# An adaptive FFN on one core: block 1 conditioned inside the first product, the first ternary quarter cut in two, and the steps of the first stage put in another order

## The reference, cut to what matters

```python
w = weights[conditions]                        # (128, 64, 64), one matrix per batch row
c = jnp.einsum('bct,bcd->bdt', x, w)           # x: (128, 64, 512)
def ternarize(W):                              # W1 (2048, 512) and W2 (512, 2048)
    delta = 0.05 * max(abs(W)); mask = abs(W) > delta
    alpha = sum(where(mask, abs(W), 0)) / max(sum(mask), 1)
    return alpha * sign(W) * mask
h = gelu(c @ ternarize(W1).T + b1)             # 2048 wide
y = h @ ternarize(W2).T + b2
scale = max(abs(y)) / 7 + 1e-8                 # one scale for all of y
out = x + clip(round(y / scale), -7, 7) * scale
```

## Time and profile before

| | us |
|---|---|
| median of 3 runs | 1014.92 (1014.45 to 1015.22) |
| the profiled execution | 1013.76 |
| its span | 1012.0 |
| PE busy | 928.2 (92%) |
| DVE busy | 647.5 (64%) |
| ACT busy | 546.2 (54%) |
| POOL busy | 145.4 (14%) |

### The profile page before, as it was taken

The page is one execution under the profiler, slowest core; times in us unless marked ns, Lnnn a source line. Parts: engine busy times, 40 slices in busy tenths (PEclk is TensorE's granted clock), DMA queues, the critical chain, the costliest instruction groups (busy, mean ns, idle before and its releaser), DMA issues.

```text
span 1012.0 us, 14566 instructions
## 1 busy us (share of the span) xinstructions
PE 928.2 (92%) x5088; PEld 439.1 (43%) x5088; DVE 647.5 (64%) x1025; ACT 546.2 (54%) x688; POOL 145.4 (14%) x187
## 2 busy tenths in 40 slices
PE   2899999999999999999999999999999999999600
PEld 2354444444444444444444444444444444444200
DVE  7999666566667666665667666565666665633492
ACT  5685826455472827446372827446372826535290
POOL 1420030210303030110303030110303030000000
PEclk9999999999999999999999999999999999999855
DMA  9401201111210301121210301121210301105899
GB/s 347 136 9 38 46 11 42 47 47 41 52 41 17 76 10 41 46 47 41 52 41 10 83 10 41 45 48 41 52 41 10 75 18 42 42 0 201 300 394 391
DMA packets 24317, 77.85 MB, mean 77 GB/s; under 512 B 3952, under 2 KB 4080, under 8 KB 23792
## 3 DMA queue, kind: packets, MB, share of 16 engines
q1 hardware_dynamic: 20032, 73.41, 24.1%
q0 software_dynamic: 3840, 3.94, 1.4%
q10 hardware_dynamic: 432, 0.34, 0.1%
HBM read 60.89 MB, written 16.78 MB: 77 GB/s over the span
## 4 chain that ended last, share of the span: by engine, by line
PE 83%; issue 9%; DVE 4%; ACT 1%; DMA 1%; DVEq 0%; POOL 0%; POOLq 0%
PE ps L426 41%; PE ps L436 36%; PE ps L491 3%; PE ps L406 3%; ACT y L680 1%; DVE st L814 1%; DVE wts L1017 1%; DMA condb<-in_itok_B 1%; DVE y L1017 0%; DVE y L833 0%; PE ps L414 0%; PE ps L454 0%; DVE yc L746 0%; DVEq L58 0%; DVE st L697 0%
## 5 line engine op out<-in xcount | busy, mean ns | idle before, releaser
L426 PE MATMUL ps<-yc,wts 128*128 128x512 f16 x2048 | 446.3, 380 | 3.6 <-DVE yc L746 3.6
L436 PE MATMUL ps<-wts 128*128 128x512 f16 x1792 | 391.4, 379 | 0.0
L426 PEld LDWEIGHTS ps<-yc,wts 128*128 128x128 f16 x2048 | 200.7, 98 | 246.8 <-DVE yc L746 4.1
L730 DVE SCALAR_TENSOR_TENSOR wts<-g,st,wts 128x512 f16<-128x512 f32 x256 | 186.3, 749 | 144.0 <-ACT wts L593 142.4
L588 ACT ACTIVATE g<-ps,b1t,st 128x512 f32<-128x512 f32 x256 | 197.9, 773 | 129.0 <-PE ps L426 120.7
L436 PEld LDWEIGHTS ps<-wts 128*128 128x128 f16 x1792 | 173.4, 98 | 204.9
L593 ACT ACTIVATE wts<-g,st 128x512 f16<-128x512 f32 x256 | 180.8, 712 | 0.0
L575 ACT ACTIVATE xs<-yx,st 128x2048 f16<-128x2048 f32 x28 | 56.1, 2002 | 135.5 <-DVE st L764 135.5
L359 POOL PARTITION_ALL_REDUCE st<-st x46 | 22.7, 494 | 672.5 <-DVE st L699 412.7
L343 POOL DMA_INDIRECT wg<-in_L_cond_weights,ids x112 | 110.0, 982 | 41.5 <-issue 29.1
L735 DVE SCALAR_TENSOR_TENSOR y<-ps,st,b2b 128x512 f32 (+1 forms) x56 | 41.6, 747 | 78.9 <-PE ps L436 78.1
(11 more groups left out here) (127 smaller groups left out, 359.3 us busy)
## 6 DMA issues: line engine op xcount, KB each, us to landing
yx<-in_x SPq DMA_DIRECT2D x56, 512.0 KB, 6.2
out<-wts SPq DMA_DIRECT2D x12, 512.0 KB, 14.9
wts<-in_x SPq DMA_DIRECT2D x10, 512.0 KB, 5.6
y<-in_L_ffn_W SPq DMA_DIRECT2D x8, 512.0 KB, 8.6
wts<-in_x SPq DMA_DIRECT2D x4, 1024.0 KB, 5.2
y<-in_L_ffn_W SPq DMA_DIRECT2D x4, 1024.0 KB, 18.5
y<-in_x SPq DMA_DIRECT2D x4, 1024.0 KB, 10.7
out<-y SPq DMA_DIRECT2D x4, 1024.0 KB, 15.3
```

The lines of the kernel that those rows point to most:

```text
L426: last = nc.tensor.matmul(psH[:, j % HB, :], T1T[:, j // HC, k, j % HC * P:(j % HC + 1) * P], csp[:, a, k, :], start=(k == 0 and a == 0), ...
L436: last = nc.tensor.matmul(psY[:, r % 2, :], hsp[:, a, j, r * P:(r + 1) * P], T2T[:, j, :], start=(j == 0 and a == 0), stop=(j == HT - 1 an ...
L730: nc.vector.scalar_tensor_tensor(out=hsp[:, 1, j, :], in0=g[:, j % HB, :], scalar=s_h, in1=hsp[:, 0, j, :], op0=ALU.mult, op1=ALU.subtract ...
```

## The change

It touches the part ahead of the loop alone. On the way to the first product: the maximum of |x| of block 0, taken by DVE, becomes a sum of |x| on ACT (with the factor 2·KT of the bound turned to 2/P); all eight `absolute` stand ahead of `spread_w(0)`; two clears go ahead of the wait for the conditions; POOL gathers half of block 1's weights at once and half behind the maximum of W1; x of block 1 is loaded ahead of W2. The first ternary quarter is made in two parts, tile 0 ahead of `low_c0` and tiles 1 to 3 behind it; `ternary1(1)` and `ternary1(2)` move ahead of the chain that makes `hscale_ready`. Block 1 is conditioned on PE between tile 0 and tile 1 of the first product, and ACT copies its c out beside tiles 3 and 5, to a place of its own in y. `relu2(0)` moves from behind the 16 gelus of block 0 to behind `gelu(0, 11)`. `count2` becomes 64 matmuls with the mask as weights and one moving column, where it was 16 with 512 columns. `low_x(0, 0)` moves from ahead of the stores of y of block 0 to behind the maxima that follow them.

```diff
@@ SP
             load_direct(0)
+            load_direct(1)
             load_weight(w2s, W2.rearrange("p j n -> p (j n)"), WCH, w2_loaded)
-            load_direct(1)
@@ POOL
-            gather_direct(0)
+            gather_direct(0, range(RT))
+            gather_direct(1, range(0, 2))
             all_max(max1_part, 1, m1r, m1, max1_all)
+            gather_direct(1, range(2, RT))
+            pool.wait_ge(x0_summed, 1)
             all_max(xwb_part, 1, xwbr, xwb, xwb_all)
-            gather_direct(1)
@@ PE
             def count2(c):
-                for n in range(WCH):
-                    last = nc.tensor.matmul(psN2, twos[:, :], quarter(neg2, c, n), start=(c == 0 and n == 0),
+                for n in range(QUARTER // P):
+                    at = c * QUARTER + n * P
+                    last = nc.tensor.matmul(psN2, neg2[:, at:at + P], twos[:, 0:1], start=(c == 0 and n == 0),
...
                 first(0, j, wait_bank=j >= HB, wait_c=False)
-            pe.wait_ge(xdirect_loaded[1], 16)
-            pe.wait_ge(w_spread, 2)
-            condition_direct(1, 0, psC)
-            pe.wait_ge(g_made, HT - 2)
-            condition_direct(1, 1, psC1)
+                if j == 0:
+                    pe.wait_ge(xdirect_loaded[1], 16)
+                    pe.wait_ge(w_spread, 2)
+                    condition_direct(1, 0, psC)
+                    condition_direct(1, 1, psC0)
+            pe.wait_ge(c_copied, 2)
             pe.wait_ge(g_made, HT)
@@ ACT
+            nc.scalar.activation(dump_x, xdirect[0].rearrange("p r t -> p (r t)"), ACT.Abs, accum_out=xwb[:, 0:1])\
+                .then_inc(x0_summed, 1)
...
-            for c in range(3):
-                relu1(c)
+            relu1(0)
             high_c0(0, psC)
             high_c0(1, psC0)
+            relu1(1)
+            act.wait_ge(c_made, 2)
+            spread_w(1)
+            relu1(2)
             relu1(3)
             act.wait_ge(relu_summed, WCH)
-            hidden(0, lambda j: spread_w(1) if j == 3 else None, wait_c=False)
...
+            def beside_first(j):
+                if j in (3, 5):
+                    copy_c_direct(1, (j - 3) // 2, (psC, psC0)[(j - 3) // 2])
+                if j == 11:
+                    act.wait_ge(delta2_ready, 1)
+                    act.wait_ge(t1_made, WCH)
+                    for side in range(2):
+                        relu2(0, side)
+            hidden(0, beside_first, wait_c=False)
@@ DVE
-            mask_w1(1)
             dve.wait_ge(wd_gathered[0], 16 * RT)
-            nc.vector.tensor_reduce(xwb[:, 1:2], wg[:, 0:RT, :], AX.XY, ALU.max, apply_absolute_value=True)
-            dve.wait_ge(xdirect_loaded[0], 16)
-            nc.vector.tensor_reduce(xwb[:, 0:1], xdirect[0], AX.XY, ALU.max, apply_absolute_value=True).then_inc(xwb_part, 1)
+            nc.vector.tensor_reduce(xwb[:, 1:2], wg[:, 0:RT, :], AX.XY, ALU.max, apply_absolute_value=True).then_inc(xwb_part, 1)
+            mask_w1(1)
             mask_w1(2)
...
             mask_w1(3)
-            ternary1(0)
+            ternary1(0, slice(0, 1), t1_begun)
             dve.wait_ge(cscale_ready, 1)
             low_c0(0, psC)
             low_c0(1, psC0)
+            ternary1(0, slice(1, HC))
+            dve.wait_ge(n1_counted, 1)
+            nc.vector.tensor_reduce(n1, psN1, AX.X, ALU.add).then_inc(n_read, 1)
+            ternary1(1)
+            ternary1(2)
             dve.wait_ge(relu_summed, WCH)
             nc.vector.tensor_reduce(rs1s, rs1, AX.X, ALU.add).then_inc(sum1_part, 1)
...
-            ternary1(1)
+            ternary1(3)
             low_h(0, 0)
...
+            for c in range(WCH):
                 last = max_w2(c)
+                low_h(0, 2 * c + 1)
+                if c < WCH - 1:
+                    low_h(0, 2 * c + 2)
...
             max_y(0, r, tile_y(r), slot(r), wait_last=r > 0)
+            low_x(0, 0)
             hidden_step(0, link, False)
```

More of the change, by code:

```diff
@@ L143, in build @@
         cf = g[:, :, :]
+        cf1 = y[:, 4, :, :]
+        dump_x = hsp[:, 0, 0:RT, :].rearrange("p j r -> p (j r)")
         def place(ap):
@@ L345, in gather, with gather_direct @@
                         in_offset=bass.IndirectOffsetOnAxis(ap=ids[:, j:j + 1], axis=0)).then_inc(w_gathered[j // HALF], 16)
-            def gather_direct(b):
-                for r in range(RT):
+            def gather_direct(b, tiles):
+                for r in tiles:
                     nc.gpsimd.indirect_dma_start(
@@ L468, in _ @@
             for j in range(HT):
-                pe.wait_ge(t1_made, j // HC + 1)
+                if j == 0:
+                    pe.wait_ge(t1_begun, 1)
+                else:
+                    pe.wait_ge(t1_made, j // HC + 1)
                 if j == HB - 1:
@@ L557, in copy_c_direct @@
                 act.wait_ge(c_made, 2 * b + half + 1)
-                nc.scalar.activation(cf[:, :, half_rows(half)], bank, ACT.Copy).then_inc(c_copied, 1)
+                nc.scalar.activation(cf1[:, :, half_rows(half)], bank, ACT.Copy).then_inc(c_copied, 1)
             def high_c0(half, bank):
@@ L833, in mask_w1, with ternary1, part @@
                 nc.vector.tensor_scalar(quarter(mask1, c), quarter(w1abs, c), dl1, 0.5, ALU.is_gt, ALU.mult).then_inc(mask1_made, 1)
-            def ternary1(c):
+            def ternary1(c, tiles=slice(0, HC), made=t1_made):
+                def part(ap):
+                    return quarter(ap, c).rearrange("p (k h) -> p k h", k=KT)[:, :, tiles.start * P:tiles.stop * P]
                 dve.wait_ge(mask1_made, c + 1)
-                nc.vector.scalar_tensor_tensor(out=quarter(t1_flat, c), in0=quarter(w1s, c), scalar=dl1, in1=quarter(mask1, c),
-                                               op0=ALU.is_gt, op1=ALU.subtract).then_inc(t1_made, 1)
+                nc.vector.scalar_tensor_tensor(out=part(t1_flat), in0=part(w1s), scalar=dl1, in1=part(mask1),
+                                               op0=ALU.is_gt, op1=ALU.subtract).then_inc(made, 1)
             mask_w1(0)
+            dve.wait_ge(wd_gathered[0], 16 * RT)
+            nc.vector.tensor_reduce(xwb[:, 1:2], wg[:, 0:RT, :], AX.XY, ALU.max, apply_absolute_value=True).then_inc(xwb_part, 1)
             mask_w1(1)
-            dve.wait_ge(wd_gathered[0], 16 * RT)
-            nc.vector.tensor_reduce(xwb[:, 1:2], wg[:, 0:RT, :], AX.XY, ALU.max, apply_absolute_value=True)
-            dve.wait_ge(xdirect_loaded[0], 16)
-            nc.vector.tensor_reduce(xwb[:, 0:1], xdirect[0], AX.XY, ALU.max, apply_absolute_value=True).then_inc(xwb_part, 1)
             mask_w1(2)
@@ L882, in ternary2 @@
                                                op0=ALU.is_gt, op1=ALU.subtract, accum_out=at2[:, c:c + 1]).then_inc(t2_made, 1)
-            ternary1(1)
+            ternary1(3)
             low_h(0, 0)
-            ternary1(2)
-            low_h(0, 1)
-            low_h(0, 2)
-            max_w2(0)
-            low_h(0, 3)
-            low_h(0, 4)
-            ternary1(3)
-            for c in range(1, WCH):
-                low_h(0, 2 * c + 3)
-                low_h(0, 2 * c + 4)
+            for c in range(WCH):
                 last = max_w2(c)
+                low_h(0, 2 * c + 1)
+                if c < WCH - 1:
+                    low_h(0, 2 * c + 2)
             link(last)
             nc.vector.tensor_reduce(mx2, wm2, AX.X, ALU.max).then_inc(max2_part, 1)
-            low_h(0, 11)
+            low_h(0, 8)
             dve.wait_ge(max2_all, 1)
@@ L903, in _ @@
             dve.sem_inc(delta2_ready, 1)
+            dve.wait_ge(relu_summed, WCH)
             ternary2(0)
-            for j in range(12, HT):
+            for j in range(9, 12):
                 low_h(0, j)
             ternary2(1)
-            max_c(1, link)
+            low_h(0, 12)
             ternary2(2)
+            low_h(0, 13)
+            max_c(1, link, cf1)
+            ternary2(3)
+            for j in range(14, HT):
+                low_h(0, j)
             nc.vector.tensor_scalar(ph0, ph, 1.0 / TOP, None, ALU.mult)
@@ L912, in _ @@
             scale_h(1, link)
-            low_c(1)
-            ternary2(3)
-            max_xw(0, 0, DIRECT)
+            low_c(1, cf1)
+            dve.wait_ge(n2_counted, 1)
+            nc.vector.tensor_copy(at2[:, WCH:], psN2).then_inc(n2_read, 1)
             dve.wait_ge(t2_made, WCH)
+            dve.wait_ge(n2_read, 1)
             nc.vector.tensor_reduce(sum2[:, 1:2], at2, AX.X, ALU.add)
```

64 lines of the change are left out of this document (25 added, 39 removed).

## The result

| | before | changed |
|---|---|---|
| median of 4 runs each, us | 1014.68 (1013.52 to 1015.22) | 1021.09 (1020.19 to 1021.79) |
| ratio, 95% interval | | 1.007 (1.0057 to 1.0083) |
| the profiled execution (its span), us | 1013.76 (1012.0) | 1021.79 (1019.9) |

The changed kernel is slower by 0.7%, 6.4 us in the medians. The profiled execution of it is the slowest of its four, and that of the kernel before lies 0.9 under its median, so the traces differ by 7.9 (spans).

A forecast was written before the change was run, and what follows sets the result against it. PE was taken as the bound, with no slack in the loop. An earlier start of block 1's first product (-0.9) and the moved low_x (+6.9) gave +6.0 on 1013.76, 1019.8, plus 1.16 for the median: 1021.0 us, range 1016.5 to 1025.0.

The forecast's parts named there:

- The loop has no slack: In the loop PE is busy all 720 us from 180 to 900, so gains or losses ahead reach the end one for one.
- Start of the first product, 28.7: Block 0's first product starts at 28.7, 4.4 us earlier, at full clock; bounds 28.7, for PE's own list, to 29.9.
- GpSimd beside VectorE: Ahead of the first product, POOL's gathers are slowed beside DVE by a shared SBUF interface; one took 1.95 us.
- The late bound of 24.7: Two gathers ahead of POOL's reduction could push the scale's chain from 23.1 to 24.7 and the first product to 29.9.
- hscale_ready, delta2 and relu2: Block 0: hscale_ready 38.3, delta2 56.1, two relu2 done 60.1, last gelu 64.7; PE idle 4.7 us before the second product.
- my first rival: No hold before block 0's second product, early start kept: saves 3.6 and 1.7, so +0.7, 1015.7 us; chance 0.06.
- The low clock, 1.7 behind each pause: PE's matmuls behind the pauses before block 0's second product and in block 1's first product lose 1.7 us each.
- my upper bound of 2.5: Most that the low clock was to cost behind the pause before block 0's second product: 2.5 us, lower bound 0.
- count2, 2.2 us: Ahead of block 1's first product, 64 count2 matmuls take 2.2 us, 1.4 saved; bounds 1.1 and 7.5 us.
- S, 96.2: Start of block 1's first product: 97.05 - 1.2 + 1.7 - 1.4 = 96.2, 0.9 earlier than before.
- low_x moved, 6.9: Late load of x makes PE wait 5.2 us at tile 10 of block 1's first product, plus 1.7 low clock: 6.9.
- Sum, +6.0: Whole kernel: -0.9 + 6.9 = +6.0 on the execution's 1013.76, so 1019.8; plus 1.16 for the median, 1021.0.

The follow-up runs named there:

- run 2: Changed kernel with maximum, scale and low_x of half block 0 ahead of DVE's wait for count2, POOL's two reductions swapped: 1012.12 us, ratio 0.9975 to the kernel before.
- run 3: Changed kernel with the first two relu2 put back behind the 16 gelus of block 0: 1018.79 us, ratio 1.0045 to the kernel before.
- run 6: Changed kernel with matmuls on constants, results unused, in both pauses of PE, waits left alone: 1024.9 us against 1021.20 for the kernel before, ratio 1.0038.
- run 5: Kernel before with only low_x(0, 0) moved behind the stores and maxima of y of block 0: 1028.24 us against 1021.20, ratio 1.0063.
- run 8: Kernel of run 4 with low_h of tiles 9 to 11 between the two instructions of ternary2(0): 1015.18 us against 1021.20 for the kernel before, ratio 0.9937.
- run 9: Kernel of run 8 with alpha's chain ahead of low_x on DVE: 1007.15 us against 1014.09 for the kernel before, ratio 0.9935.
- run 4: Changed kernel with the edits of run 2 and run 3 together: 1011.27 us, ratio 0.9971 to the kernel before.
- run 7: Changed kernel, load of x left late, look at half block 1 and its high and low parts later: 1018.29 us against 1021.20 for the kernel before, ratio 0.997.
- run 1: Changed kernel with low_x(0, 0) alone put back ahead of the stores of y of block 0: 1014.15 us, ratio 0.9997 to the kernel before.
- run 10: Kernel of run 9 with the first two relu2 kept behind gelu 11 of block 0: 1011.46 us, ratio 0.9971 to the kernel before.

## Why the prediction was right, point by point

- **The loop has no slack, so PE's timeline ahead of it is the sum.** Shown: 887.2 and 887.3 us behind the loop's start.
- **Start of the first product, 28.7.** Measured 29.21, in the other runs of the changed start 28.5 to 29.5. In the changed kernel PE's own list did set it, but condition took 6.69 us and not 5.49 (5.5 to 6.7 in these runs; why is not shown). My bound, not before 28.7, did not hold: in run 2 PE began condition at 19.20 and the product at 28.51, released by DVE's low_c0. The full clock in the product came as said.
- **GpSimd beside VectorE.** The reduction stands behind the two gathers and began at 22.95, when the second ended; DVE, done with its masks, waited 0.52 us for it, so the scale's chain began at 23.32 for my 23.1 and hung on GpSimd, where I had it hang on DVE. It did not reach PE, which was at the counts until 29.2. The late bound of 24.7 was not met. With the rule of the Trainium skill behind that bound (GPSIMD Engine Reference, "1. Specifications") the trace agrees: the two gathers took 1.59 and 2.41 us beside DVE's masks, the one before them, beside a maximum of W1, 0.94:

```profile
14.95 0.94 POOL L353 DMA_INDIRECT wg<-in_L_cond_weights,idsd  x1 [0.30 <-issue]
...
18.62 1.59 POOL L353 DMA_INDIRECT wg<-in_L_cond_weights,idsd  x1 [0.21 <-issue]
...
20.51 2.41 POOL L353 DMA_INDIRECT wg<-in_L_cond_weights,idsd  x1 [0.30 <-issue]
...
22.95 0.34 POOL L364 PARTITION_ALL_REDUCE st<-st  x1
```

- **hscale_ready, delta2 and relu2.** 37.9 for 38.3; 55.7 for 56.1; 59.7 for 60.1; the 16th gelu 64.3 for 64.7. The pause was 3.8 us for 4.7, since PE got there 0.5 later and left 0.4 earlier. What I missed is that DVE's order held the gelus almost as long (run 3). That did not touch the forecast, but my first rival, which let the whole hold go with relu2, was priced wrongly: run 3 gave 2.3 us in the medians, not 5.3, since the pause of 3.28 us stayed.
- **The low clock, 1.7 behind each pause.** The mechanism is shown by run 6. The sizes were 2.6 and 1.9, so this term of the sum was too small; for the pause ahead of the second product my upper bound of 2.5 was passed.
- **count2, 2.2 us.** 1.74, 27 ns a pair of weight load and matmul. The sequencer path of about 62 ns a matmul in the Trainium skill (TensorE: Matmul & The Clock Gate, "Step-by-step: what each phase is for") is not what happens here; its section "Wait — 56ns, not 53.3ns?" states a floor of about 25 ns between starts, and with that the trace agrees.
- **S, 96.2.** 96.19, by luck: the errors cancel, the second product 0.4 earlier, 0.9 more low clock, 0.5 less for count2.
- **low_x moved, 6.9.** On the kernel before, alone, it is right (run 5: 6.7). In the profiled execution of the change it was 8.9: the load took 8.8 us from its issue to DVE's look and not 7.3, so the pause was 6.95 for 5.2. This term is mis-sized there. The waits and their order are those that I described. From its issue to DVE's look the load took 7.1 to 8.8 us where DVE waited for it (runs 5, 6, 3 and the change: 7.1, 7.3, 8.0, 8.8); why it varies is not shown.
- **Sum, +6.0.** Medians +6.4, 1021.09 for my 1021.0. That the two are so close is luck. The sum is told on the profiled execution, and there it was 2.0 too small (1019.8 for 1021.79), nearly all of it in the term of low_x. I then added the 1.16 us by which the medians of the kernel before lay over its profiled execution; in the changed kernel the median lies 0.7 under it.
- **Not told apart:** the price of each early edit (sum on ACT, split quarter, order of masks). Only their joint start, 3.9 us earlier, is measured. The old count2 in the new order was not run; its 1.9 us is read from the traces.

## What to carry to other kernels

An instruction that frees a buffer for a load belongs ahead of everything that has slack, and the first reader of that load belongs where nothing urgent stands behind it; either of the two is enough. Before filling a dense stage with work on an engine that feeds it, walk the list of every engine from the new item to the next thing that PE waits for: here two items of 4 and 3.6 us, each harmless by the busy shares (ACT 54%, DVE 64%), held the same last gelus of block 0. A pause of PE has a second price behind it, so price it twice.

## What the runs showed of the hardware that I had not expected

The low clock behind a pause has no fixed price. Ahead of the second product it was, pause and extra time over 20.88: 0.92 us and 0 (run 8); 1.17 and 0 (run 9); 2.87 and 1.3 (run 4); 3.28 and 0 (run 3); 3.79 and 2.6 (changed); 4.06 and 1.7 (run 7); 4.30 and 1.5 (run 2); 4.31 and 1.6 (run 1); 4.31 and 1.7 (run 10). Each is one execution. From 2.87 us on, a longer pause was not always dearer than a shorter one. The time of one kernel goes with the granted clock: in run 10 the two executions at a mean granted clock of 0.973 took 1010.12 and 1010.20 us, the five at 0.970 to 0.972 took 1011.12 to 1012.23. With matmuls on constants in the pause the price was 0 (run 6: 20.89 us; in block 1's pause 0.1).

A half block of x is loaded by two transfers of 512 KB, issued some 0.7 us apart, and they do not land alike: in the changed kernel the first landed 5.0 us after its issue and the second 8.1, in run 5 4.9 and 6.3. So DVE's look came 8.8 us after the first issue in the changed kernel, 7.1 in run 5 (105.34 to 112.43), and in run 1 at most 7.0.
